# Norm and head projection of a dense attention joined in one block, chunk by chunk

## The chip, the cores and the metric

One core of one Trainium2 chip. The metric is the device time of one execution in microseconds (us). Engines: PE is TensorE, PEld its weight loads, DVE is VectorE, ACT is ScalarE, POOL is GpSimd, SP is SyncE, which here only issues DMAs.

## What is computed

Two transformer layers on x of 2 x 1024 tokens by 128 channels. In each, a condition vector gives shift, scale and gate for two parts, and each part adds its gated result to x. The first part of a layer is a dense attention of 16 heads of 8 dimensions, and it begins with what matters here:

```python
h = _layernorm(x, axis=-1) * (1 + ca) + sa
# layer 0: rotary attention
qkv = (x @ w_qkv.T + b_qkv)          # x is h here
q = elu(q) + 1; k = elu(k) + 1       # then the rotary turn of the pairs
# layer 1: causal attention
q = embedded @ Wq.T + bq; k = embedded @ Wk.T + bk; v = embedded @ Wv.T + bv
v = jnp.where(jnp.isnan(v), 0.0, v)
```

After them follow a windowed attention with a feed-forward part (layer 0) and a mixture of experts (layer 1).

## The kernel before

x lies with channels on the 128 partitions and the 2048 tokens along them, in four chunks of 512. `build` (L2181) runs: `prologue`, then for the first dense attention `layer_norm` (call at L2214), `project_heads` (L2215) and `attention` (L2216), then the windowed layers, then `causal_block` (L1599) with the same three calls (L1604, L1607, L1608), then the experts. Each of these functions is one block: all engines meet at its end before any begins the next.

`layer_norm` (L213). Per chunk: an average over channels as a matmul with a matrix of 1/128 (L236, all four chunks first), centring on DVE (L290), square on ACT (L266), variance per token by four one-column matmuls (L244), root on ACT (L270), reciprocal on DVE (L294), the reciprocal spread over the partitions by four matmuls with the identity (L252), rescale on DVE (L298), shift on ACT (L274), which writes h. The root needs another function table of ACT than an exponential: such a change is an ACT_TABLE_LOAD record. A float32 matmul stands in the trace as two records, so "x2" at L425 is one matmul.

`project_heads` (L364). SP loads the weights and the bias and then the rows of ones (L343); ACT asks for the three rotary tables (L464). PE, ACT and DVE begin with a wait for the weights. Then steps s = 0 to 7, each one half (q or k) of a chunk; every engine has its own order, written out, and takes its instructions strictly in it. PE: `project(s)` (L425), `swap_pairs(s-2)` (L434), on even s `project_v` (L439), on odd s `turn_v` (L447). In the rotary case DVE drains a projection twice (L515, then L516: a pair of ramps), ACT takes the exponential (L469), POOL adds (L559), PE swaps pairs, DVE multiplies by cosine (L522) and sine (L527), POOL adds (L563). The result, val, is split in three bf16 parts: hi on ACT (L478), the rest on DVE (`less_hi`, L531), mid on ACT (L482), lo on POOL (L567), each some steps behind the projection. In the second attention ACT drains the projection (`biased`, L473) and there are no ramps; DVE cleans the values (L545 to L549). The values' bias (L486) and their tokens-first copy (L492) are ACT's in both. Projections use banks 0 and 1 of PSUM, swaps 2 and 3, values 4 and 5, turned values 6 and 7.

The parts reach the attention through DRAM: SP stores hi, mid, lo of the first batch's first group once four steps of each are done (L413, L351), waits for all to land (L415) and loads the first operands (L416, L360). The rest of the stores follow in the attention's block. The attention's first matmul (L716) waits for those operands.

`ChunkNorm` (L1611) is the same norm with one method per instruction and chunk, used so far by the experts only.

## Time and profile before

| | |
|---|---|
| median of 3 runs | 1840.9 us (1837.91 to 1841.72) |
| the profiled execution's own time | 1846.47 us |
| its span, first to last instruction | 1844.7 us |
| mean granted TensorE clock | 0.919 of the full one |
| first norm | 15.2 to 31.4 us |
| rotary projection block | 31.7 to 80.0 us |
| first matmul of the first dense attention | 84.14 us |
| second norm | 951.9 to 970.4 us |
| second projection block | 970.6 to 1007.8 us |
| first matmul of the second dense attention | 1012.25 us |

All times are microseconds from the span's start. The span leaves out what lies around the instructions, so it is compared with the time of its own execution and not with the median. The timeline merges neighbouring instructions of one line: its second number is then the length of the whole group, and in brackets stands how long the engine was idle before it and what ended that.

### The profile page before, as it was taken

The numbers are of one execution on the slowest core, as the hardware profiler recorded it, in microseconds if no ns is written. First come the engines' busy times: TensorE is split into PE (matmuls) and PEld (weight loads), VectorE is DVE, ScalarE is ACT, GpSimd is POOL, SyncE is SP. The second block draws the span as 40 slices with busy tenths as digits, with TensorE's granted clock in tenths as the row PEclk, the third lists the DMA queues.
The fourth block names the chain that finished last, engine by engine and source line by source line (L and its number), as shares of the span: only waits on it lengthen the run. The fifth ranks groups of instructions, "written<-read, shape, count | busy, mean of one in ns | idle before, by whom it ended". The sixth has DMA issues, their size and how long they took to land. (4 is left out here: it accounts for less than half of the span.)

```text
span 1844.7 us, 29294 instructions
## 1 busy us (share of the span) xinstructions
PE 1571.4 (85%) x11008; PEld 858.9 (47%) x11008; DVE 1393.5 (76%) x1954; ACT 1194.9 (65%) x2308; POOL 623.7 (34%) x492
## 2 busy tenths in 40 slices
PE   6489999997689876799783899999985799999998
PEld 4112222222357653566551233333323578888886
DVE  3799999992677446775443999999944489999996
ACT  2338888886377742777424377777772577777776
POOL 1840000000477522775003222222222255555555
PEclk8769999999799978999786699999996899999999
DMA  2140000000111100111001401111002021111111
GB/s 73 60 128 19 18 19 19 18 2 9 58 33 33 28 21 18 29 31 33 1 1 51 145 19 22 21 22 22 4 7 72 1 69 44 44 47 47 47 47 52
DMA packets 66620, 66.04 MB, mean 36 GB/s; under 512 B 38920, under 2 KB 42632, under 8 KB 65968
## 3 DMA queue, kind: packets, MB, share of 16 engines
q1 hardware_dynamic: 65840, 61.94, 12.3%
q8 instruction: 88, 1.44, 0.3%
q10 hardware_dynamic: 576, 2.16, 0.3%
q14 instruction: 52, 0.43, 0.1%
q0 software_dynamic: 64, 0.07, 0.0%
HBM read 40.85 MB, written 14.81 MB: 30 GB/s over the span
## 5 line engine op out<-in xcount | busy, mean ns | idle before, releaser
L817 ACT ACTIVATE att_probs<-psum 128x512 f32<-128x512 f32 x1024 | 535.2, 604 | 202.9 <-PE psum L745 202.3
L828 DVE TENSOR_REDUCE att_neg_max<-psum 128x1 f32<-128x1024 f32 x512 | 600.9, 1219 | 45.1 <-PE psum L716 39.3
L716 PE MATMUL psum<-att_k_op,att_q_op 48*128 48x512 bf16 x1024 | 351.0, 409 | 56.2 <-DMA att_k_op<-qk_parts 34.6
L745 PE MATMUL psum<-att_q_op,att_k_op 50*128 50x512 bf16 x1024 | 314.2, 388 | 19.4 <-ACT att_probs L817 19.4
L1916 ACT ACTIVATE moe_hidden<-psum,moe_b 128x512 f32<-128x512 f32 x256 | 167.4, 690 | 83.2 <-PE psum L76 83.0
L69 DVE TENSOR_TENSOR moe_hidden_low<-moe_hidden,moe_hidden_high 128x512 fp32r<-128x512 f32 x192 | 203.9, 1110 | 5.3 <-ACT moe_hidden_high L1922 5.2
L763 PE MATMUL psum<-att_probs,att_v 128*32 128x512 f32 (+2 forms) x1664 | 203.4, 558 | 2.9 <-ACT att_sums L809 2.8
L745 PEld LDWEIGHTS psum<-att_q_op,att_k_op 50*128 50x128 bf16 x1024 | 78.2, 94 | 250.9 <-ACT att_probs L817 187.6
L904 POOL TENSOR_TENSOR att_diag<-att_probs,att_triangle 128x512 f32<-128x512 f32 x64 | 82.0, 1281 | 272.5 <-PE psum L766 176.6
L716 PEld LDWEIGHTS psum<-att_k_op,att_q_op 48*128 48x128 bf16 x1024 | 72.5, 95 | 180.7 <-DVE att_neg_max L828 120.5
L1977 POOL TENSOR_TENSOR moe_hidden_low<-moe_hidden,moe_hidden_high 128x512 fp32r<-128x512 f32 x64 | 94.8, 1482 | 167.2 <-ACT moe_hidden_high L1922 167.2
L1433 POOL TENSOR_TENSOR wl_qk<-wl_qk,wl_part 128x512 f32<-128x512 f32 x64 | 81.5, 1276 | 88.4 <-DVE wl_part L1367 88.4
L1972 POOL TENSOR_TENSOR moe_cur<-moe_cur,moe_term 128x512 f32<-128x512 f32 x64 | 105.8, 1653 | 13.9 <-DVE moe_term L2052 13.6
L74 PE MATMUL psum<-moe_hidden_high,moe_w_high 128*128 128x512 f32 x256 | 103.4, 404 | 5.9 <-DVE moe_hidden_low L69 5.9
L1922 ACT ACTIVATE moe_hidden_high<-moe_hidden 128x512 fp32r<-128x512 f32 x192 | 106.6, 625 | 0.0
L74 PE MATMUL psum<-moe_cur_high,moe_w_high 128*128 128x512 f32 x256 | 101.6, 397 | 0.0
L76 PE MATMUL psum<-moe_hidden_high,moe_w_low 128*128 128x512 f32 x256 | 100.9, 394 | 0.0
L75 PE MATMUL psum<-moe_hidden_low,moe_w_high 128*128 128x512 f32 x256 | 100.7, 393 | 0.0
L1384 DVE TENSOR_REDUCE wl_mx<-psum 128x4 f32<-128x512 f32 x64 | 44.1, 689 | 73.9 <-PE psum L1185 73.9
L76 PE MATMUL psum<-moe_cur_high,moe_w_low 128*128 128x512 f32 x256 | 99.9, 390 | 0.0
L75 PE MATMUL psum<-moe_cur_low,moe_w_high 128*128 128x512 f32 x256 | 99.7, 390 | 0.0
L893 POOL COPY att_v<-v_tok 128x256 f32<-128x256 f32 x16 | 6.4, 399 | 253.5 <-PE psum L763 253.4
(239 smaller groups left out, 2897.8 us busy)
## 6 DMA issues: line engine op xcount, KB each, us to landing
moe_spread_weights<-gate_rows SPq DMA_DIRECT2D x64, 256.0 KB, 3.2
wl_v_shift<-wl_v SPq DMA_DIRECT2D x62, 128.0 KB, 2.2
att_q_op<-qk_parts SPq DMA_DIRECT2D x32, 192.0 KB, 3.2
att_k_op<-qk_parts SPq DMA_DIRECT2D x32, 192.0 KB, 4.3
qk_parts<-att_hi SPq DMA_DIRECT2D x12, 256.0 KB
qk_parts<-att_hi SPq DMA_DIRECT2D x12, 192.0 KB
qk_parts<-att_mid SPq DMA_DIRECT2D x8, 256.0 KB
moe_w<-in_moe_w SPq DMA_DIRECT2D x2, 1024.0 KB, 8.5
```

Of the source, the lines that this page charges most:

```text
L69: return dve.tensor_tensor(dst, src, high.bitcast(F32), ALU.subtract)
L74: pe.matmul(out, w_high, x_high, start=start, stop=False)
L75: pe.matmul(out, w_high, x_low, start=False, stop=False)
L76: return pe.matmul(out, w_low, x_high, start=False, stop=stop)
L716: mm = pe.matmul(buf[:, half * CHUNK:(half + 1) * CHUNK], q_op[it % RING][at_rows(p, MAX_ROW), j, t * P:(t + 1) * P], k_op[it % RING][at_r ...
L745: pe.matmul(st_bank[e % 3], k_op[it % RING][at_rows(p, MAX_ROW + 2), j, t * P:(t + 1) * P], q_op[it % RING][at_rows(p, MAX_ROW + 2), j, ha ...
L763: last = pe.matmul(out[:, 0:full], stage_v[r][:, t, j, :], pr[:, 0:full], start=first_tile, stop=final and full == CHUNK, skip_group_check ...
L817: act.activation(probs[:, g % PB, h, :], st_bank[e % 3], ACT.Exp, scale=scale).then_inc(exp_done, 1)
L828: dve.tensor_reduce(neg[:, t, p, j:j + 1], ring[e % 2], AX.X, ALU.max, negate=True).then_inc(ring_free, 1)
L1916: act.activation(hidden[:, n % 2, f, :], k.psum[:, f, :], ACT.Gelu_apprx_tanh, bias=b1[:, e, f:f + 1]).then_inc(gelu_done, 1)
L1922: act.activation(hidden_high[:, n % 2, f, :], hidden[:, n % 2, f, :], ACT.Copy)\
L1972: pool.tensor_tensor(cur[:, at], cur[:, at], term[:, n % 2, :], ALU.add).then_inc(added, 1)
```

## The change

`project_heads` takes x and the scale and shift and calls a `ChunkNorm` itself; the calls of `layer_norm` ahead of both dense attentions go. So norm and projection are one block, twice. The weights, the rotary tables and the rows of ones are asked for at its head, beside the norm; the wait for the weights stands behind the norm's first pieces. Chunk 0 and most of chunk 1 are normed ahead of step 0; the rest of chunk 1 lies in steps 0 and 1, and chunks 2 and 3 lie between the steps up to 5. `project(s)` on even s waits for its chunk's shift. The norm takes banks 6 and 7, so the values go through bank 4 alone and the turned values through bank 5 alone. `ChunkNorm` moves up in the file as it is (its removed copy is cut below).

```diff
--- before.py
+++ after.py
@@ -315,6 +315,67 @@
                                              ALU.mult, ALU.add)
 
 
+class ChunkNorm:
+
+
+    def __init__(self, nc, k, tag, src, dst, room, banks, scale, shift):
+        self.k, self.src, self.dst, self.scale, self.shift = k, src, dst, scale, shift
+        self.d, self.sq, self.dev, self.inv = room
+        self.at = [slice(c * CHUNK, (c + 1) * CHUNK) for c in range(CHUNKS)]
+        self.tiles = [slice(4 * c, 4 * c + 4) for c in range(CHUNKS)]
+        self.bank = [k.psum[:, b, :] for b in banks]
+        (self.mean, self.centred, self.squared, self.var, self.rooted, self.inverse, self.spread, self.scaled,
+         self.shifted) = sems(nc, *(f"{tag}_{n}" for n in LN_SEMS))
+
+    def average(self, pe, c):
+        pe.matmul(self.bank[c], self.k.ones_mean[:, :], self.src[:, self.at[c]], start=True, stop=True)\
+          .then_inc(self.mean, 1)
+
+    def centre(self, dve, c):
+        dve.wait_ge(self.mean, c + 1)
+        dve.tensor_tensor(self.d[:, self.at[c]], self.src[:, self.at[c]], self.bank[c], ALU.subtract)\
+           .then_inc(self.centred, 1)
+
+    def square(self, act, c):
+        act.wait_ge(self.centred, c + 1)
+        act.activation(self.sq[:, self.at[c]], self.d[:, self.at[c]], ACT.Square).then_inc(self.squared, 1)
+
+    def variance(self, pe, c):
+        pe.wait_ge(self.squared, c + 1)
+        for t in range(4):
+            i = 4 * c + t
+            last = pe.matmul(self.bank[c][:, t:t + 1], self.sq[:, i * P:(i + 1) * P], self.k.ones_mean[:, 0:1],
+                             start=True, stop=True)
+        last.then_inc(self.var, 1)
+
+    def root(self, act, c):
+        act.wait_ge(self.var, c + 1)
+        act.activation(self.dev[:, self.tiles[c]], self.bank[c][:, 0:4], ACT.Sqrt, bias=self.k.eps[:, 0:1])\
+           .then_inc(self.rooted, 1)
+
+    def invert(self, dve, c):
+        dve.wait_ge(self.rooted, c + 1)
+        dve.reciprocal(self.inv[:, self.tiles[c]], self.dev[:, self.tiles[c]]).then_inc(self.inverse, 1)
+
+    def spread_inverse(self, pe, c):
+        pe.wait_ge(self.inverse, c + 1)
+        for t in range(4):
+            i = 4 * c + t
+            last = pe.matmul(self.bank[c][:, t * P:(t + 1) * P], self.inv[:, i:i + 1].broadcast_to([P, P]),
+                             self.k.ident[:, :], start=True, stop=True)
+        last.then_inc(self.spread, 1)
+
+    def rescale(self, dve, c):
+        dve.wait_ge(self.spread, c + 1)
+        dve.scalar_tensor_tensor(self.d[:, self.at[c]], self.d[:, self.at[c]], self.scale(c * CHUNK // SEQ),
+                                 self.bank[c], ALU.mult, ALU.mult).then_inc(self.scaled, 1)
+
+    def add_shift(self, act, c):
+        act.wait_ge(self.scaled, c + 1)
+        act.activation(self.dst[:, self.at[c]], self.d[:, self.at[c]], ACT.Identity,
+                       bias=self.shift(c * CHUNK // SEQ)).then_inc(self.shifted, 1)
+
+
 class OperandRing:
 
 
@@ -361,7 +422,7 @@
                              self.parts[which, b, g, p].rearrange("c d j t -> (c d) j t")).then_inc(self.loaded[r], 16)
 
 
-def project_heads(nc, k, tag, h, A, rotary, operands):
+def project_heads(nc, k, tag, x, h, scale, shift, A, rotary, operands):
 
 
 
@@ -380,6 +441,9 @@
 
         w = sb("w", [P, 3 * DIM])
         bias = sb("b", [P, 3])
+        norm = ChunkNorm(nc, k, f"{tag}_ln", x, h, (sb("centred_x", [P, TOK]), sb("square", [P, TOK]),
+                                                   sb("deviation", [P, TILES]), sb("inverse", [P, TILES])),
+                         [6, 7, 6, 7], scale, shift)
         val = sb("val", [P, NU, CHUNK])
         part = operands.part
         if rotary:
@@ -417,9 +481,9 @@
 
         @block.tensor
         def _(pe):
-            pe.wait_ge(w_in, 16 * len(loads))
-
             def project(s):
+                if s % 2 == 0:
+                    pe.wait_ge(norm.shifted, s // 2 + 1)
                 if s >= 2:
                     pe.wait_ge(drained if rotary else operand, s - 1)
                 pe.matmul(bank[s % 2], w[:, (s % 2) * DIM:(s % 2 + 1) * DIM], h[:, cols[s // 2]],
@@ -434,20 +498,26 @@
                 pe.matmul(bank[2 + s % 2], swap[:, :], val[:, s, :], start=True, stop=True).then_inc(swapped, 1)
 
             def project_v(c):
-                if c >= 2:
-                    pe.wait_ge(v_done, c - 1)
-                pe.matmul(bank[4 + c % 2], w[:, 2 * DIM:3 * DIM], h[:, cols[c]], start=True, stop=True)\
+                if c:
+                    pe.wait_ge(v_done, c)
+                pe.matmul(bank[4], w[:, 2 * DIM:3 * DIM], h[:, cols[c]], start=True, stop=True)\
                     .then_inc(v_ps, 1)
 
             def turn_v(c):
                 pe.wait_ge(v_done if rotary else v_clean, c + 1)
-                if c >= 2:
-                    pe.wait_ge(v_tok_done, c - 1)
+                if c:
+                    pe.wait_ge(v_tok_done, c)
                 for t in range(4):
-                    last = pe.transpose(bank[6 + c % 2][:, t * P:(t + 1) * P],
+                    last = pe.transpose(bank[5][:, t * P:(t + 1) * P],
                                         k.v_ch[:, c * CHUNK + t * P:c * CHUNK + (t + 1) * P], k.ident[:, :])
                 last.then_inc(v_turned, 1)
 
+            norm.average(pe, 0)
+            norm.average(pe, 1)
+            norm.variance(pe, 0)
+            norm.spread_inverse(pe, 0)
+            norm.variance(pe, 1)
+            pe.wait_ge(w_in, 16 * len(loads))
             for s in range(NU + 2):
                 if s < NU:
                     project(s)
@@ -457,12 +527,20 @@
                     project_v(s // 2)
                 if s % 2 == 1 and 3 <= s < NU + 2:
                     turn_v((s - 3) // 2)
+                if s == 0:
+                    norm.spread_inverse(pe, 1)
+                if s in (1, 3):
+                    c = (s + 3) // 2
+                    pe.wait_ge(norm.scaled, c - 1)
+                    norm.average(pe, c)
+                if s in (2, 4):
+                    norm.variance(pe, s // 2 + 1)
+                    norm.spread_inverse(pe, s // 2 + 1)
 
         @block.scalar
         def _(act):
             for dst, src in tables:
                 act.dma_start(dst, src).then_inc(tables_in, 16)
-            act.wait_ge(w_in, 16 * len(loads))
 
             def exp_low(s):
                 act.wait_ge(floored, s + 1)
@@ -483,16 +561,22 @@
 
             def v_bias(c):
                 act.wait_ge(v_ps, c + 1)
-                act.activation((k.v_ch if rotary else vraw)[:, cols[c]], bank[4 + c % 2], ACT.Identity,
+                act.activation((k.v_ch if rotary else vraw)[:, cols[c]], bank[4], ACT.Identity,
                                bias=bias[:, 2:3]).then_inc(v_done, 1)
 
             def v_tok(c):
                 act.wait_ge(v_turned, c + 1)
                 b, t0 = c // 2, c % 2 * 4
                 act.activation(k.v_tok[:, t0:t0 + 4, b * GROUPS:(b + 1) * GROUPS, :],
-                               bank[6 + c % 2].rearrange("p (t g c) -> p t g c", t=4, c=32), ACT.Copy)\
+                               bank[5].rearrange("p (t g c) -> p t g c", t=4, c=32), ACT.Copy)\
                    .then_inc(v_tok_done, 1)
 
+            norm.square(act, 0)
+            norm.root(act, 0)
+            norm.square(act, 1)
+            norm.root(act, 1)
+            norm.add_shift(act, 0)
+            act.wait_ge(w_in, 16 * len(loads))
             for s in range(NU + 4):
                 if s < NU:
                     (exp_low if rotary else biased)(s)
@@ -504,11 +588,15 @@
                     mid(s - 4)
                 if s % 2 == 1 and 3 <= s < NU + 2:
                     v_tok((s - 3) // 2)
+                if s in (1, 3, 5):
+                    norm.add_shift(act, (s + 1) // 2)
+                if s in (1, 3):
+                    norm.square(act, (s + 3) // 2)
+                if s in (2, 4):
+                    norm.root(act, s // 2 + 1)
 
         @block.vector
         def _(dve):
-            dve.wait_ge(w_in, 16 * len(loads))
-
             def ramps(s):
                 dve.wait_ge(projected, s + 1)
                 b = bias[:, s % 2:s % 2 + 1]
@@ -530,6 +618,12 @@
                 dve.wait_ge(hi_done, s + 1)
                 dve.tensor_tensor(val[:, s, :], val[:, s, :], of(part[0], s), ALU.subtract).then_inc(rest1, 1)
 
+            norm.centre(dve, 0)
+            norm.centre(dve, 1)
+            norm.invert(dve, 0)
+            norm.rescale(dve, 0)
+            norm.invert(dve, 1)
+            dve.wait_ge(w_in, 16 * len(loads))
             for s in range(NU + 4):
                 if rotary and s < NU:
                     ramps(s)
@@ -548,6 +642,14 @@
                     dve.wait_ge(sined, 2 * c + 2)
                     dve.copy_predicated(k.v_ch[:, cols[c]], same[:, cols[c]].bitcast(mybir.dt.uint32),
                                         vraw[:, cols[c]]).then_inc(v_clean, 1)
+                if s == 0:
+                    norm.rescale(dve, 1)
+                if s in (3, 5):
+                    norm.rescale(dve, (s + 1) // 2)
+                if s in (1, 3):
+                    norm.centre(dve, (s + 3) // 2)
+                if s in (2, 4):
+                    norm.invert(dve, s // 2 + 1)
 
         @block.gpsimd
         def _(pool):
@@ -1601,72 +1703,10 @@
         k.v_ch = a.enter_context(nc.sbuf_tensor("v_ch1", [P, TOK], F32))
         k.v_tok = a.enter_context(nc.sbuf_tensor("v_tok1", [P, SEQ_TILES, UNITS, 32], F32))
         k.att = a.enter_context(nc.sbuf_tensor("att1", [P, SEQ_TILES, UNITS, 32], F32))
-        layer_norm(nc, k, "ln2", k.x, h, part(1, 1), part(1, 0))
         with ExitStack() as ring:
             operands = OperandRing(nc, k, "att1", ring)
-            project_heads(nc, k, "plain", h, A, False, operands)
+            project_heads(nc, k, "plain", k.x, h, part(1, 1), part(1, 0), A, False, operands)
             attention(nc, k, "att1", 1.0 / float(np.sqrt(SEQ)), True, operands)
-
-
...
 def heads_and_experts(nc, k, A, part, h, store):
@@ -2211,8 +2251,7 @@
             with ExitStack() as ring:
                 operands = OperandRing(nc, k, "att0", ring)
                 with nc.sbuf_tensor("h0", [P, TOK], F32) as h:
-                    layer_norm(nc, k, "ln0", k.x, h, part(0, 1), part(0, 0))
-                    project_heads(nc, k, "rot", h, A, True, operands)
+                    project_heads(nc, k, "rot", k.x, h, part(0, 1), part(0, 0), A, True, operands)
                 attention(nc, k, "att0", 1.0 / float(np.sqrt(HEAD_DIM)), False, operands, lepe.convolve)
             residual_attention(nc, k, "res0", lepe)
         with scope(nc):
```

## Rows read from the trace of the kernel before

**Rows 1.** The page of the profile, part 1: busy time, share of the span, instructions.

```profile
PE 1571.4 (85%) x11008; PEld 858.9 (47%) x11008; DVE 1393.5 (76%) x1954; ACT 1194.9 (65%) x2308; POOL 623.7 (34%) x492
```

**Rows 2.** Timeline, first norm: start, us, engine, line, operation, idle before it.

```profile
18.02 0.63 ACT L266 ACTIVATE ln_square<-ln_centred_x 128x512 f32<-128x512 f32 x1 [13.33 <-DVE ln_centred_x L290]
...
20.07 1.28 ACT L270 ACT_TABLE_LOAD   x1
...
26.89 0.97 PEld L252 LDWEIGHTS psum<-ident,ln_inverse 128*128 128x128 f32 x8
...
28.09 0.75 DVE L298 SCALAR_TENSOR_TENSOR ln_centred_x<-ln_centred_x,mod,psum 128x512 f32<-128x512 f32 x1
```

**Rows 3.** Timeline, the rotary projection block, same columns.

```profile
31.69 0.33 SPq L410 DMA_DIRECT2D rot_w<-in_rot_w  x1
...
35.88 2.08 PE L425 MATMUL psum<-h,rot_w 128*128 128x512 f32 x2 [6.00 <-DMA rot_b<-in_rot_b]
...
38.07 0.75 DVE L515 TENSOR_SCALAR rot_tmp<-psum,rot_b 128x512 f32<-128x512 f32 x1 [7.40 <-PE psum L425]
...
40.15 0.75 DVE L515 TENSOR_SCALAR rot_tmp<-psum,rot_b 128x512 f32<-128x512 f32 x1 [0.67 <-PE psum L425]
...
57.32 1.13 PE L434 MATMUL psum<-rot_val,rot_swap 128*128 128x512 f32 x2 [1.47 <-POOL rot_val L559]
57.74 0.74 DVE L515 TENSOR_SCALAR rot_tmp<-psum,rot_b 128x512 f32<-128x512 f32 x1
...
62.21 0.74 DVE L515 TENSOR_SCALAR rot_tmp<-psum,rot_b 128x512 f32<-128x512 f32 x1
...
62.87 0.73 DVE L516 TENSOR_SCALAR rot_val<-psum,rot_b 128x512 f32<-128x512 f32 x1
...
66.25 2.07 PE L434 MATMUL psum<-rot_val,rot_swap 128*128 128x512 f32 x2 [3.16 <-POOL rot_val L559]
```

**Rows 4.** Windows: length, busy of PE PEld DVE ACT POOL, granted clock, DMA, GB/s.

```profile
50.00:66.00 16.00, 8.24 (x22) 3.10 (x22) 16.00 (x20) 8.01 (x14) 16.00 (x11) 0.89 0.04 12
```

**Rows 5.** Groups by line: first norm, then (from L522) the rotary block.

```profile
L298 DVE SCALAR_TENSOR_TENSOR ln_centred_x<-ln_centred_x,mod,psum 128x512 f32<-128x512 f32 x4 | 3.0, 738 | 1.1 <-PE psum L252 1.1
L274 ACT ACTIVATE h<-ln_centred_x,mod 128x512 f32<-128x512 f32 x4 | 2.9, 721 | 4.5 <-DVE ln_centred_x L298 4.5
...
L270 ACT ACTIVATE ln_deviation<-psum,eps 128x4 f32<-128x4 f32 x4 | 1.0, 249 | 0.0
L294 DVE RECIPROCAL ln_inverse<-ln_deviation 128x4 f32<-128x4 f32 x4 | 0.7, 178 | 5.5 <-ACT ln_deviation L270 5.5
...
L522 DVE TENSOR_TENSOR rot_tmp<-rot_val,rot_cos 128x512 f32<-128x512 f32 x8 | 11.0, 1369 | 0.6 <-POOL rot_val L559 0.6
...
L531 DVE TENSOR_TENSOR rot_val<-rot_val,att_hi 128x512 f32<-128x512 f32 x8 | 9.2, 1146 | 2.0 <-ACT att_hi L478 1.8
...
L482 ACT ACTIVATE att_mid<-rot_val 128x512 bf16<-128x512 f32 x8 | 5.0, 628 | 10.6 <-DVE rot_val L531 10.6
```

**Rows 6.** Timeline, norm and projection ahead of the second dense attention.

```profile
965.00 3.53 PEld L252 LDWEIGHTS psum<-ident,ln_inverse 128*128 128x128 f32 x16
...
967.17 0.75 DVE L298 SCALAR_TENSOR_TENSOR ln_centred_x<-ln_centred_x,mod,psum 128x512 f32<-128x512 f32 x1 [1.44 <-PE psum L252]
...
973.29 2.07 PE L425 MATMUL psum<-h,plain_w 128*128 128x512 f32 x2 [4.45 <-DMA plain_b<-in_plain_b]
...
975.46 0.69 ACT L473 ACTIVATE plain_val<-psum,plain_b 128x512 f32<-128x512 f32 x1 [5.09 <-PE psum L425]
...
987.76 0.66 ACT L478 ACTIVATE att_hi<-plain_val 128x512 bf16<-128x512 f32 x1
```

**Rows 7.** Timeline, the end of the rotary block: stores, last lo, operand load.

```profile
69.88 1.18 SPq L351 DMA_DIRECT2D qk_parts<-att_lo  x2
...
75.61 2.52 POOL L567 TENSOR_TENSOR att_lo<-rot_val,att_mid 128x512 bf16<-128x512 f32 x2
...
78.29 0.82 SPq L360 DMA_DIRECT2D att_q_op<-qk_parts  x2
```

48 lines of the change are left out of this document (removed).

## The prediction

> **What bounds the kernel now.** The page comes first: TensorE is busy 85% of the span [rows 1], but the change touches only two stretches of about 70 and 60 us, one ahead of each dense attention, and there no engine is busy throughout. So I read the timeline of those stretches, then the groups of instructions for durations, then the rows at the handover to the attention. The reader is to see three things. (1) The first norm is latency: small instructions of four engines in a chain [rows 2]. After it TensorE sits idle 6.00 us, and in the second dense stage 4.45 us, until the weights, asked for only at the head of the projection block, have landed [rows 3, 6]. (2) The rotary projection begins with steps of 2.1 to 4 us and ends with steps of 4.47 us (57.74 to 62.21), in which VectorE and GpSimd are both busy the whole time [rows 3, 4]. (3) The projection block ends with a transfer: the last stores are issued at 69.88, their landing is waited for until 78.29, and only then are the attention's operands asked for. GpSimd's last piece ends at 75.61 + 2.52 = 78.13, just before [rows 7]. So what counts is when the first batch's parts (steps 0 to 7) are ready for the stores; the later steps hide behind the landing.
>
> The profiled execution took 1846.47 us, 5.6 above the 1840.9 median; the sum is made in its microseconds and the difference put on the median. About 0.2% (3.7 us) is what a measurement of this kernel can tell from no change.
>
> **Heads: what is won.** Rotary. Average, centring and first square stay where they are: the square starts at 18.02 [rows 2]. The table load of the root, now behind the second square (20.07), moves behind the first: 18.7 to 20.0. Then root 0.25, reciprocal 0.18, spread to rescale 1.2 (26.89 to 28.09), variance of chunk 1 behind the spread 1.0, root(1) and shift(0) 0.25 + 0.72 [rows 2, 5]. So 20.0 + 0.25 + 0.2 = 20.45, spread issued until 21.5, variance until 22.5, root(1) until 22.8, shift(0) until 23.5. The weights, asked for at 15.2, need the 4.2 us that they need now (31.69 to 35.88 [rows 3]) and are there. Projection(0) at 23.5, and the first ramp 2.19 later (35.88 to 38.07 [rows 3]): 25.7, now 38.07, so 12.4 won. Bounds: all at half clock 11.5 (spread 2.17 instead of 1.2, 965.00 to 967.17 [rows 6]), all at full clock 13.5. Second stage, same chain from 951.9: the first biased drain falls between 961.9 and 964.5, now 975.46 [rows 6]; won 11.0 to 13.6, taken 12.2, the middle, since this stretch shows both clock levels. **Together 24.6.** Issuing weights and tables early costs nothing: SP, with its loads and the six rows of ones, is idle there, and ACT's three table issues, some 1.3 us by the 0.33 of the row at 31.69 and its like, end before its first square is due at 18.02; a copy late by x would only delay that square by x.
>
> **Inside the projection: what is paid.** Chunks 2 and 3 are now normed between the steps. Each engine takes its instructions in order, so the chain shift(c) -> projection is closed at every chunk, while now all of h lies ready. I walk from ramp to ramp, rotary (starts of a pair lie 0.66 apart, 62.21 and 62.87 [rows 3]).
> Step 0: now 2.08 (38.07 to 40.15); spread(1) stands in TensorE's queue ahead of projection(1), 0.97 of issue [rows 2]: 3.05.
> Step 1: ramp 0.74, exponential 0.63, shift(1) 0.72, projection(2) 1.13 (57.32 [rows 3]), handovers: 3.45. Centring(2), 0.7 on VectorE, lies beside it.
> Step 2: swap and values behind projection(2), estimated 0.8 each from the 1.13 less its fill, then value bias 0.7, table load 1.28, root 0.25, reciprocal 0.18, spread 0.97, projection(3) 1.13, handovers 0.2: 6.3. VectorE waits, since projection(3) stands behind spread(2) and that behind the reciprocal.
> Step 3: ramps 1.3, cosine 1.0 (0.7 alone to 1.37 beside GpSimd [rows 5]), sine 0.65, rescale(2) 0.74, shift(2) 0.72, projection(4) 1.13: 5.5.
> Step 4: ramps 1.3, cosine 1.0, sine 0.6, less_hi(0) 1.05; then on ACT, ahead of root(3), mid(0) 0.63 and the table load 1.28; root, reciprocal, spread, projection(5) 0.25 + 0.18 + 0.97 + 1.13, handovers 0.2: 8.6.
> Step 5: to the end of less_hi(1) 3.95, mid(1) and value tokens 1.05, shift(3) 0.72, projection(6) 1.13, handovers 0.2: 7.1.
> Step 6 has no norm: 4.47 as now, or down to 2.9 as GpSimd has no backlog; taken 3.6.
> Sum 37.6; now 24.14 (38.07 to 62.21 [rows 3]): **13.5 paid**. To it comes the clock. In step 4 TensorE has nothing from variance(3) to spread(3), about 3.9 us, and after an idle 3.16 us the pair of matmuls at 66.25 took 2.07 where the one at 57.32 took 1.13 [rows 3]. I put spread(3) and projection(5) at half clock: 1.0 + 0.95 = **2.0**. Bounds 0, and 6 if every norm matmul and projection of steps 2 to 5 on the path falls so.
> Second stage (no exponentials: the root's table stays, no load is added), from one biased drain to the next, by the same kind of chain with ACT pieces at 0.5 to 0.6 when they stand behind one another. Step 0: values at half clock, spread and projection(1), 1.9 + 1.1 + 1.1 = 4.1. Step 1: drain, shift, projection, 0.7 + 0.7 + 1.1, and centring's handovers 0.5 = 3.0. Step 2: values, variance 0.8 + 0.7, root 0.25, reciprocal 0.18, spread, projection 0.97 + 1.13 = 4.0. Step 3: drain, hi, value tokens, shift on ACT 2.4, projection 1.13 = 3.55. Step 4: values 0.85, hi(1), mid(0), root(3) 1.4, reciprocal, spread, projection 2.28, the value drain and handovers 0.65 = 5.2. Step 5: drain, hi, mid, tokens, shift 2.85, projection 1.13 = 4.0. Then value bias and hi(3) 2.05, where the stores begin. Sum 25.9; now 975.46 to 987.76 + 0.66 = 12.96 [rows 6]: **12.9 paid**. Its idle gaps of TensorE stay near 1 to 2 us, so no clock term; bounds 0 and 4.
>
> Four more table loads (two before roots, two before exponentials) cost 1.28 each [rows 2]; the two before exponentials lie in ACT's wait for the next ramp and cost nothing, unless ACT is late there, then 1.28 each. Values in one bank cost nothing: bias(c-1) has drained the bank two steps before values(c); without that cover each would wait 0.7. The joined block saves one barrier, contained in the absolute times. After lo(3) the stores, landing and loads are the same, and GpSimd ends before SP can even ask for the operands [rows 7].
>
> A load took 1.28 us in the row (20.07), with the root 1.30 behind it, and the walk uses that. The Trainium skill's page ScalarE: Activation LUTs (What ACT_TABLE_LOAD costs, and Table sets) wants activations grouped by table set and budgets about 2.7 us for every switch, drain included. It speaks against this interleaving; by its figure the two loads on the path would cost 2.8 us more. The row shows half the figure, so the page's direction is kept, its size not.
>
> Sum: -24.6 + 13.5 + 2.0 + 12.9 = **+3.8 us**: 1844.7.
>
> **Rivals.**
> A, faster: the stalls thin out the work, so VectorE and GpSimd no longer slow each other. The cosine takes 1.37 in the mean and less_hi 1.15 [rows 5], and about 0.7 either would take alone; in steps 4 to 6 that gives back 3 x (0.7 + 0.45) = 3.5. With it, and no half clock, and nothing else: 3.8 - 3.5 - 2.0 = -1.7; with heads at full clock another 2.5 off: -4.2, 1836.7. For it: both engines are full in 50 to 66 [rows 4]. Against: ACT's and TensorE's chain, not VectorE, ends steps 2 to 5. Chance 0.14.
> B, slower by the clock: TensorE runs at half clock (1.2 GHz) through steps 2 to 5 of both stages, deciding wherever its gap reaches 3 us. Price 6 - 2 = 4 more in the first, 4 in the second: +11.8, 1852.7; one stage alone 1848.7. For it: the matmuls at 66.25 and the spread at 965.00 are at half clock [rows 3, 6]. Against: over 50 to 66, with TensorE busy 8.24 of 16 us, the granted clock is still 0.89 of the full one [rows 4]. The Trainium skill's page TensorE: Matmul & The Clock Gate (What's actually happening) has 1.2 GHz as the state to which an idle TensorE falls back; by that rule, the trace agrees (2.07 against 1.13). Chance 0.16.
> C, the change is hidden: the stores' landing (8.4 us) is set by the queue and not by their issue, or the shifts of steps cancel; within 0.2%. Chance 0.1.
> D, ACT is the late one: the loads before exponentials are not hidden, 2 x 1.28, and the two roots wait as long again: +3.8 + 2.6 to 5.1, 1847 to 1850. Chance 0.1.
>
> **How the numbers follow.** The forecast has 0.5, its own range is 0 to +7 us (1841 to 1848), cut by the 3.7 about in the middle: 0.27 within, 0.23 slower. B 0.16 and D 0.1 are slower, but a third of them, a small dose, ends within: 0.09. A is 0.14 faster, C 0.1 within. Sum: faster 0.14, within 0.46, slower 0.40. The range takes in the forecast, most of A and B with one stage, and the bounds of the heads (2.5) and the clock: 1837.5 to 1852.
>
> **What would show it.** Right: first ramp at about 25.7; ramps of steps 2, 3 and 5 apart by 6, 5.5 and 7 us; VectorE idle before them on TensorE; six table loads where now two are; the first operand load of the attention 3 us later in the first stage, under 1 later in the second. Wrong if step 4 takes under 6 us (A) or over 10 (B, D), if the first ramp is later than 28, or if the attention's first matmul moves otherwise than the eighth ramp.

## The result and the profile after

| | before | after |
|---|---|---|
| median of the runs | 1840.9 us (1837.91 to 1841.72) | 1850.21 us (1847.71 to 1855.74) |
| ratio, 95% interval | | 1.0059 (1.0039 to 1.0078) |
| the profiled execution's own time | 1846.47 us | 1847.71 us |
| its span | 1844.7 us | 1845.9 us |
| first matmul, first dense attention | 84.14 us | 89.65 us |
| second norm's first matmul to second attention's first | 60.34 us | 59.87 us |

The change makes the kernel slower, by 9.3 us on the medians and by 0.59% of 1841, 10.9 us, by the ratio. The forecast was 3.8 us slower, so its size was 5.5 us too small. The measured time lies in the stated range (1837.5 to 1852), and "slower" had 0.40 against 0.46 for "within 0.2%".

The two profiled executions differ by only 1.2 us. This pair understates the change: the one before is a long one of its kind and the one after the shortest of its five. So single spans are compared here only stretch by stretch, and totals by ratios.

The page of the kernel after, part 1, answers to [rows 1]; it tells as little as it did then.

```profile
PE 1578.2 (85%) x11008; PEld 861.1 (47%) x11008; DVE 1387.5 (75%) x1954; ACT 1200.8 (65%) x2312; POOL 622.3 (34%) x492
```

The timeline of the first stage after (start, us, engine, line, operation, idle before and what ended it) answers to [rows 2] and [rows 3]. L603 is the first ramp of a step, L489 the projection, L364 the spread, L353 the root.

```profile
23.53 2.04 PE L489 MATMUL psum<-h,rot_w 128*128 128x512 f32 x2 [1.05 <-ACT h L375]
...
25.69 0.75 DVE L603 TENSOR_SCALAR rot_tmp<-psum,rot_b 128x512 f32<-128x512 f32 x1 [2.70 <-PE psum L489]
...
30.16 0.75 DVE L603 TENSOR_SCALAR rot_tmp<-psum,rot_b 128x512 f32<-128x512 f32 x1 [0.39 <-PE psum L489]
...
49.31 1.28 ACT L353 ACT_TABLE_LOAD   x1
...
51.14 2.07 PE L364 MATMUL psum<-ident,rot_inverse 128*128 128x128 f32 x8 [3.73 <-DVE rot_inverse L358]
...
53.00 1.92 PE L489 MATMUL psum<-h,rot_w 128*128 128x512 f32 x2
...
54.96 0.75 DVE L603 TENSOR_SCALAR rot_tmp<-psum,rot_b 128x512 f32<-128x512 f32 x1 [3.87 <-PE psum L489]
...
60.45 2.08 PE L489 MATMUL psum<-h,rot_w 128*128 128x512 f32 x2 [3.28 <-ACT h L375]
...
66.17 0.74 DVE L603 TENSOR_SCALAR rot_tmp<-psum,rot_b 128x512 f32<-128x512 f32 x1
```

The reader is to see the first ramp at 25.69 (it was 38.07), and step 4, from 44.94 to 54.96: ACT's table load at 49.31, then spread and projection in a row at half clock (2.07 and 1.92 us; in step 2, at full clock, 1.16 and 1.02), with VectorE idle 3.87 us in front of the ramp. Between 25.7 and 66.2 VectorE waited 14.4 us for projections, 3.7 for roots and 1.9 for a spread.

The same timeline at the handover, SP's queue and the attention's first matmul, answers to [rows 7]:

```profile
66.08 3.67 SPq L412 DMA_DIRECT2D qk_parts<-att_hi  x6
...
71.41 2.40 SPq L412 DMA_DIRECT2D qk_parts<-att_mid  x4
...
73.85 1.18 SPq L412 DMA_DIRECT2D qk_parts<-att_lo  x2
...
83.76 0.82 SPq L421 DMA_DIRECT2D att_q_op<-qk_parts  x2
...
89.65 1.04 PE L818 MATMUL psum<-att_k_op,att_q_op 48*128 48x512 bf16 x4 [16.55 <-DMA att_k_op<-qk_parts]
```

and in a second profile of the kernel before (experiment e0):

```profile
60.76 3.67 SPq L351 DMA_DIRECT2D qk_parts<-att_hi  x6
...
70.03 1.18 SPq L351 DMA_DIRECT2D qk_parts<-att_lo  x2
...
78.43 0.82 SPq L360 DMA_DIRECT2D att_q_op<-qk_parts  x2
```

The eighth ramp came 3.96 us later (66.17 against 62.21), the lo stores 3.97 later (73.85 against 69.88), but the operand loads 5.47 later (83.76 against 78.29). That difference is explained below: what counts is the first hi store.

The second stage after, which answers to [rows 6]; it begins at 954.30, 2.39 us later than before:

```profile
959.46 1.16 PE L364 MATMUL psum<-ident,plain_inverse 128*128 128x128 f32 x8 [0.67 <-DVE plain_inverse L358]
...
964.61 0.69 ACT L551 ACTIVATE plain_val<-psum,plain_b 128x512 f32<-128x512 f32 x1 [2.29 <-PE psum L489]
...
990.84 3.66 SPq L412 DMA_DIRECT2D qk_parts<-att_hi  x6
...
1014.17 1.04 PE L818 MATMUL psum<-att_k_op,att_q_op 48*128 48x512 bf16 x4 [18.56 <-DMA att_k_op<-qk_parts]
```

The first biased drain comes 10.31 us after the norm's first matmul (before 23.55), the hi stores 36.54 after it (before 36.53) and the attention's first matmul 59.87 (before 60.34; e0 59.86). Here the head's win of 13.2 us is spent to the last tenth by the time of the first hi store.

### The profile page after: what moved, and what is told of

The parts are those of the page before. It is cut to its first block and busy times, and to the rows that moved or that the text cites. A ratio compares the mean times of both kernels' runs of the same rounds, so it can differ in the third digit from the quotient of the medians.

```text
span 1845.9 us, 29282 instructions
## 1 busy us (share of the span) xinstructions
PE 1578.2 (85%) x11008; PEld 861.1 (47%) x11008; DVE 1387.5 (75%) x1954; ACT 1200.8 (65%) x2312; POOL 622.3 (34%) x492
## 5 line engine op out<-in xcount | busy, mean ns | idle before, releaser
L847 PE MATMUL psum<-att_q_op,att_k_op 50*128 50x512 bf16 x1024 | 314.2, 387 | 19.5 <-ACT att_probs L919 19.5
L1535 POOL TENSOR_TENSOR wl_qk<-wl_qk,wl_part 128x512 f32<-128x512 f32 x64 | 81.6, 1277 | 88.6 <-DVE wl_part L1469 88.5
```

The costliest lines, as they stand in the source:

```text
L847: pe.matmul(st_bank[e % 3], k_op[it % RING][at_rows(p, MAX_ROW + 2), j, t * P:(t + 1) * P], q_op[it % RING][at_rows(p, MAX_ROW + 2), j, ha ...
```

## Experiments

Each kernel ran with the kernel of before on the same chip. Ratios are to that one, with 95% intervals; stretches come from the profile of the run named.

### e0 and e1: both kernels once more

No edit.

> The kernel of before once more, as one of the kernels under test. The medians moved by 9.3 us while the two profiled executions differ by 1.2 us in span. If the profiled execution of before (span 1844.7, 1846.5 us) was only a long one of its kind, a second profile has a span near 1839 (time near 1841), with the difference spread over stretches that the change does not touch. If profiling itself lengthens the execution by 5 us, it comes out near 1844.7 again while its timed runs stay near 1841. Ratio to before: 1.000 within 0.001.

> The changed kernel once more. The chain theory (steps closed by the norm's chain cost more than the heads save) expects the first attention's first matmul again 5 to 6 us later than before and the second attention's start relative to its norm 0.5 us earlier than before, so about +2 to +5 in all. A rival, that something outside the two joined stretches became slower (a later phase of the clock or of transfers in the windowed layers), expects these two stretches as just said, but the time 9 us above before, with the excess in the windowed layers, the attentions or the experts.

Before: 1842.4 us, ratio 1.0007 (0.9992 to 1.0022), span 1840.9. The first profile of before was indeed a long one: from the first matmul of its first attention (L716) to the first score matmul (L745) it took 31.0 us, this one 29.2, and the experts' part 448.3 against 446.4. After: 1852.2 us, ratio 1.0059 (1.0038 to 1.0080), span 1852.6: the same ratio twice, so the loss is firm, and larger than the +2 to +5 us expected here.

The first attention begins at 90.09 (e0: 84.09), 6.0 us later. The second stage took 63.22 us from its norm's first matmul to the attention's, 3.4 more than in e0 and 3.35 more than in the first profile of the changed kernel. Of these 3.35, 2.57 are there at the first hi store (39.11 us after the norm's first matmul, for 36.54), and they come with TensorE's clock in the head, as the timeline of e1 shows; the other 0.8 lies behind the stores.

```profile
962.40 2.08 PE L364 MATMUL psum<-ident,plain_inverse 128*128 128x128 f32 x8 [0.57 <-DVE plain_inverse L358]
...
969.18 0.69 ACT L551 ACTIVATE plain_val<-psum,plain_b 128x512 f32<-128x512 f32 x1 [2.29 <-PE psum L489]
```

The spread took 2.08 us where the profile above had 1.16; the variances before and after it took 1.80 and 1.71 for 1.06 and 0.96. The first biased drain came 12.69 us after the norm's first matmul instead of 10.31. What decides between the two levels was not found.

The rival of e1, that something outside the two stages became slower, is not borne out: from the first attention's first matmul to the second norm's it is 866.4 us here and 864.7 in the profile after, for 867.8 and 867.3 in the two of before.

### e2 and e3: one stage joined at a time

```diff
 # e2: causal_block
+        layer_norm(nc, k, "ln2", k.x, h, part(1, 1), part(1, 0))
...
-            project_heads(nc, k, "plain", k.x, h, part(1, 1), part(1, 0), A, False, operands)
+            project_heads_apart(nc, k, "plain", h, A, False, operands)   # the old function
 # e3: build, the same for the rotary stage, and causal_block as changed
```

> Only the rotary stage is joined; the second dense attention has the separate norm and projection of before. Chain theory: the first stage carries the loss (+5.5 at its handover by the trace, of which the attention gives back about 2), the second nothing, so this is slower than before by 2 to 6 us and as slow as the full change within 1 us. Rival (the second stage or something behind it carries the rest): +2 to +3 here, and the other half with the second stage alone.

> Only the second dense stage is joined; the rotary one is as before. Chain theory: within 1 us of before (0.5 us faster by the trace: the steps have no table loads and no half clock). Rival: slower by 4 us or more, which would put the missing part of the 9 us here.

First only: 1850.0, ratio 1.0050 (1.0033 to 1.0067), +9.2 us; the first attention begins at 91.15. Second only: 1845.6, ratio 1.0019 (1.0005 to 1.0034), +3.5 us; the second stage took 62.67 us, again with the head at half clock (first drain after 12.70). The first stage carries most of the loss, more than the 2 to 6 us expected: its first attention begins 7.1 us later than in e0, where I had counted on 5.5, of which the attention was to give back 2. The second was expected within 1 us of before and is not free: up to the first hi store it loses nothing when its head runs at full clock and 2.6 us when not. Four of seven profiles with a joined second stage that is otherwise that of the change had the head at 12.7 (e1, e3, g2, g3), three at 10.3 (after, f4, and f2 at 10.20).

### f1: the norm ahead of the steps, in the joined block

```diff
-                         [6, 7, 6, 7], scale, shift)
+                         [4, 5, 6, 7], scale, shift)
 # tensor (scalar and vector likewise, in layer_norm's order)
-            norm.average(pe, 0)
-            norm.average(pe, 1)
-            norm.variance(pe, 0)
-            norm.spread_inverse(pe, 0)
-            norm.variance(pe, 1)
+            for c in range(CHUNKS):
+                norm.average(pe, c)
+            for c in range(CHUNKS + 1):
+                if c < CHUNKS:
+                    norm.variance(pe, c)
+                if c:
+                    norm.spread_inverse(pe, c - 1)
 # in the steps: no norm; project(2) also waits for the last rescale;
# values in banks 4 and 5, turned values in 6 and 7, as before
```

> The joined block with the weights asked for at its head, but all four chunks normed ahead of step 0 in the order of the old norm, and the values in two banks as before. Chain theory (the loss is what is interleaved, the gain is the weights' wait): projection(0) starts when TensorE has issued spread(3), about 30 us in the first stage against 35.9 before and some 17.5 us after the norm's start in the second against 21.4; the steps are as before. So 5 to 6 us won in the first stage, 4 in the second: 9 to 10 us faster than before, some 18 to 20 faster than the full change. Rival (the joined block itself, its early transfers or its memory layout is what costs): no faster than before.

1831.7, ratio 0.9945 (0.9928 to 0.9963): 10.1 us faster than before and about 21 faster than the full change. Timeline of its first stage:

```profile
29.80 1.91 PE L491 MATMUL psum<-h,rot_w 128*128 128x512 f32 x2
...
31.83 0.75 DVE L595 TENSOR_SCALAR rot_tmp<-psum,rot_b 128x512 f32<-128x512 f32 x1 [1.04 <-PE psum L491]
...
54.38 3.67 SPq L412 DMA_DIRECT2D qk_parts<-att_hi  x6
...
72.06 0.82 SPq L421 DMA_DIRECT2D att_q_op<-qk_parts  x2
...
77.80 1.04 PE L806 MATMUL psum<-att_k_op,att_q_op 48*128 48x512 bf16 x4 [14.85 <-DMA att_k_op<-qk_parts]
```

The projection starts at 29.8 (before 35.88) and the steps keep their old lengths (24.15 us to the eighth ramp; before 24.14). The second stage took 54.07 us. So joining the blocks and asking early is worth 12 us at the two handovers, and norming between the steps is what loses: this kernel differs from the changed one in that placement (and in the values' banks, which cost nothing, as shown below).

### f2: the spread behind the next projection

```diff
                 if s < NU:
                     project(s)
+                if s in (3, 5):
+                    norm.spread_inverse(pe, (s + 1) // 2)
...
                     norm.variance(pe, s // 2 + 1)
-                    norm.spread_inverse(pe, s // 2 + 1)
```

> The changed kernel with one thing moved: spread(2) and spread(3) stand in TensorE's queue behind projection(3) and projection(5) and not ahead of them. Chain theory: steps 2 and 4 of the rotary stage lose the spread and the projection from their path and last 4.1 and about 6 us where the change has 6.3 and 10.0, since only the reciprocal holds VectorE; 6 us won at the first stage's stores, and about 4 (steps 2 and 4, 2 each) in the second if ACT is not the next limit there; time 4 to 8 us below the full change. Rival (ACT's root with its table loads sets the steps anyway): under 2 us won.

1846.6, ratio 1.0020 (1.0010 to 1.0031): some 7 us below the full change's ratio. Steps 2 and 4 of the rotary stage lasted 4.11 and 6.06 us (expected 4.1 and about 6). The timeline shows the ramp right behind the reciprocal, and where part of it is given back:

```profile
39.59 0.18 DVE L358 RECIPROCAL rot_inverse<-rot_deviation 128x4 f32<-128x4 f32 x1 [1.40 <-ACT rot_deviation L353]
...
39.68 0.72 DVE L604 TENSOR_SCALAR rot_tmp<-psum,rot_b 128x512 f32<-128x512 f32 x1
...
57.87 1.26 PE L489 MATMUL psum<-h,rot_w 128*128 128x512 f32 x2 [2.35 <-ACT h L375]
...
59.17 0.75 DVE L604 TENSOR_SCALAR rot_tmp<-psum,rot_b 128x512 f32<-128x512 f32 x1 [2.45 <-PE psum L489]
```

Step 5 (51.25 to 59.17) lasts 7.9 us in place of 7.6 and ends on ACT's shift: the next projection still waits for chunk 3 of h. From the first to the eighth ramp it is 35.28 us for 40.48. In the second stage step 5 grows from 4.03 to 7.76 and eats the 4 us won in steps 2 and 4. TensorE's order costs about what I said; behind it stands the chain of the norm itself.

### f4: TensorE kept busy in step 4

```diff
                     norm.variance(pe, s // 2 + 1)
+                    if s == 4:
+                        for _ in range(4 if rotary else 0):
+                            pe.matmul(bank[6], k.ones_mean[:, :], x[:, cols[0]], start=True, stop=True)
                     norm.spread_inverse(pe, s // 2 + 1)
```

> The changed kernel with four matmuls of no use (their output is overwritten) on TensorE between variance(3) and spread(3) of the rotary stage, where it idles 3.7 us. If the half clock there costs what the forecast put on it, spread(3) and projection(5) take 1.2 and 1.1 instead of 2.1 and 2.0 and step 4 lasts 8.1 instead of 10.0, and projection(6) may follow at full clock, another 1.0: 2 to 3 us below the full change. If the useless matmuls delay what they stand ahead of, or the level falls regardless, 0 or slower by up to 1.

```profile
49.55 3.68 PE L540 MATMUL psum<-x_ch,ones_mean_sb 128*128 128x512 f32 x8
...
53.42 1.16 PE L364 MATMUL psum<-ident,rot_inverse 128*128 128x128 f32 x8 [0.19 <-DVE rot_inverse L358]
...
54.42 1.02 PE L489 MATMUL psum<-h,rot_w 128*128 128x512 f32 x2
...
55.48 0.75 DVE L606 TENSOR_SCALAR rot_tmp<-psum,rot_b 128x512 f32<-128x512 f32 x1 [2.11 <-PE psum L489]
```

With the four useless matmuls (L540), spread(3) took 1.16 and projection(5) 1.02, at full clock, and step 4 lasted 8.25 us in place of 10.02. So the half clock there costs 1.8 us; the forecast had 2.0. Step 5 stayed at 7.60. The first ramp of this run came at 28.04, and its step 2 lasted 7.05 us for 6.30, as in g2 (7.05), which has none of these matmuls: projection(3) took 1.77 there in both, for 1.02. The ratio, 1.0041 (1.0023 to 1.0059), is 3 us below the change's 1.0059, but the intervals overlap: shown is the step, not the total.

### f5: hi's stores later, in the kernel of before

```diff
-                sp.wait_ge(part_done, NU // BATCH)
+                sp.wait_ge(part_done, NU // BATCH + (1 if level == 0 else 0))
```

> The kernel of before, but in both stages the stores of hi wait for one more step (five instead of four); mid and lo as before. In the first stage of five profiles the operands were asked for 17.7 us after the first hi store in each, though the lo stores came 9.3 us after it in two of them and 7 to 8 in three. If the transfers' own length, counted from the first store, sets the landing, the hi stores, about 3.5 us later in the first stage and 2 in the second, move the first attention matmul by as much: 5 us slower in all. If the last store sets it, only what the queue pushes lo back counts, about 1 us in the first stage and 1 in the second: under 2 us slower.

```profile
64.76 3.67 SPq L351 DMA_DIRECT2D qk_parts<-att_hi  x6
...
70.92 2.15 SPq L351 DMA_DIRECT2D qk_parts<-att_lo  x2
...
82.44 0.82 SPq L360 DMA_DIRECT2D att_q_op<-qk_parts  x2
```

The first hi store came at 64.76, 4.0 later than in e0, and the loads at 82.44: 17.68 us after it, although the lo stores came only 0.9 later than in e0 (70.92 against 70.03). In the second stage the hi stores moved by 1.90 and the loads by 1.91. Ratio 1.0028 (1.0014 to 1.0042), 5.2 us, as expected if the landing is counted from the first store. The same 17.68 us (17.66 to 17.69) stands between first hi store and operand load in both stages of every profile of a kernel with these stores, while the lo stores stand 8.4 to 11.5 us ahead of the load. Divided by the 12 stores it is 1.47 us each, the start and the last landing counted in.

### g3: no table loads inside the steps

```diff
+class PlainRootNorm(ChunkNorm):
+    def root(self, act, c):
+        if c < 2:
+            return super().root(act, c)
+        act.wait_ge(self.var, c + 1)
+        act.activation(self.dev[:, self.tiles[c]], self.bank[c][:, 0:4], ACT.Identity, bias=self.k.eps[:, 0:1])\
+           .then_inc(self.rooted, 1)
```

> The changed kernel, but for chunks 2 and 3 of the rotary stage ACT leaves the square root out (it passes the variance through an Identity of the same size), so that no function table changes inside the steps: only the root of those chunks is not computed. A load is 1.28 us in each trace. If it is on the path once per chunk at that price, steps 2 and 4 of the rotary stage shorten by 1.3 each (6.3 to 5.0, 10.0 to 8.7), more in step 4 if TensorE's shorter pause keeps it at full clock: 2.5 to 4.5 us at the handover. By the 2.7 us a switch of the Trainium skill's page ScalarE: Activation LUTs (What ACT_TABLE_LOAD costs) the two steps would shorten by 2.7 each, 5.4 in all. If the loads are hidden, nothing changes.

The kernel leaves out the square root of chunks 2 and 3 in the rotary stage; the rest is as in the change.

```profile
49.74 0.25 ACT L384 ACTIVATE rot_deviation<-psum,eps 128x4 f32<-128x4 f32 x1
...
50.25 1.27 PE L364 MATMUL psum<-ident,rot_inverse 128*128 128x128 f32 x8 [2.30 <-DVE rot_inverse L358]
...
53.27 0.75 DVE L612 TENSOR_SCALAR rot_tmp<-psum,rot_b 128x512 f32<-128x512 f32 x1 [3.07 <-PE psum L498]
```

Step 2 lasted 5.08 us (change 6.30), so the load cost 1.22 there. Step 4 lasted 7.79 (10.02): 2.23 less, of which 1.28 is the load; TensorE's spread, 1.27 us for 2.07, was still at full clock after the shorter pause. The projection behind it was not (1.92). So one load is on the path per interleaved root, at 1.2 to 1.3 us. The Trainium skill's page ScalarE: Activation LUTs (What ACT_TABLE_LOAD costs) gives 1.28 us for the load and 1.38 for a drain with it, 2.66 for a switch. The trace agrees with the first figure; with the drain on the path too, step 2 would have shortened by 2.66, and it shortened by 1.22. The head of this run was 2.2 us later (first ramp 27.91), and its step 6 lasted 4.61 us for 3.61, which hides the gain in the total: ratio 1.0047 (1.0032 to 1.0063), not distinguishable from the change's.

### g4: the weights late again, norm ahead of the steps

```diff
 # sync, in f1
+            sp.wait_ge(norm.shifted, CHUNKS)
             for dst, src in loads:
                 sp.dma_start(dst, src).then_inc(w_in, 16)
 # scalar: the tables' issues moved behind the same wait
```

> The version with the norm ahead of the steps, but weights, bias and tables are asked for only once the last chunk is shifted, as before the change. If that version's gain (12 us at the two handovers) is the weights' wait and the overlap that it allows, this one is back at the kernel of before: within 1 us of it. If the joined block gives something by itself (no barrier, another order), 1 to 5 us of the gain stay.

```profile
31.41 0.33 SPq L475 DMA_DIRECT2D rot_w<-in_rot_w  x1
...
34.42 2.07 PE L492 MATMUL psum<-h,rot_w 128*128 128x512 f32 x2 [4.58 <-DMA rot_b<-in_rot_b]
```

1840.1, ratio 0.9998 (0.9981 to 1.0015). The first attention begins at 81.6, 3.8 us later than in f1, and the second stage takes 58.19 for 54.07, 4.1 more. So about 8 of f1's 12 us at the handovers are the weights asked for early (here TensorE again sits 4.58 us for a transfer of 3.0), with the overlap of projection(0) and the last shifts. Against e0 the two handovers together still look 4 us better; the ratio's interval reaches from -3.5 to +2.8 us, so whether the joined block by itself gives anything stays open.

### g1 and g2: the first portion's stores cut in two

```diff
+                if portion == 0:
+                    for p in range(2):
+                        rows = slice(p * 2 * HEAD_DIM, (p + 1) * 2 * HEAD_DIM)
+                        sp.dma_start(self.parts[which, b, 0, p, c].rearrange("d j t -> (d j) t"),
+                                     self.part[level][rows, which, b * SEQ:(b + 1) * SEQ])\
+                          .then_inc(self.stored[portion], 16)
+                    continue
```

> The version with the norm ahead of the steps, and each store of the first portion cut into its two groups of 16 rows, so that the outermost dimension of the destination is 16 and not 2. In the traces so far these stores move at a steady 50 GB/s with a DMA share of 0.13, which is 2 of 16 engines, and the operands are asked for 17.68 us after the first of them in every profile. The Trainium skill's page DMA: Bandwidth & Descriptors (Why a DMA increments its semaphore by 16) says that a transfer is spread over the largest number of engines up to 16 that divides the slowest dimensions, 2 here. If that is the cause, the 24 shorter stores are bound by their issue: at 0.45 to 0.6 us each 11 to 14.4 us, and 2 to land, so 13 to 16.4 instead of 17.7: 1.3 to 4.5 us won in each of two stages, 3 to 9 in all against the version without. Rival (the transfers are bound by something else, such as the writes to DRAM): the share stays at 0.13 and nothing is won, or the issues of 24 stores cost more than 17.7: slower.

> The changed kernel with the same cut of the first portion's stores. If hi's stores set the handover because two engines carry all of them, then with 16 engines the operand load waits for lo and its landing: the loads are asked for 13 to 16.4 us after the first hi store instead of 17.7, 3 to 9 us below the full change. Rival: no difference.

Timeline of g1, SP's queue and the attention's first matmul:

```profile
53.16 5.44 SPq L415 DMA_DIRECT2D qk_parts<-att_hi  x12
...
63.57 1.81 SPq L415 DMA_DIRECT2D qk_parts<-att_lo  x4
...
66.63 0.77 SPq L428 DMA_DIRECT2D att_q_op<-qk_parts  x2
...
72.36 1.04 PE L813 MATMUL psum<-att_k_op,att_q_op 48*128 48x512 bf16 x4 [10.63 <-DMA att_k_op<-qk_parts]
```

The windows from the first store to the landing (length, busy time of PE, PEld, DVE, ACT, POOL, granted clock, DMA share, GB/s) of the change and of g2:

```profile
66.10:83.70 17.60, 4.61 (x13) 1.74 (x11) 11.91 (x13) 7.60 (x13) 15.85 (x11) 0.72 0.12 45
```

```profile
69.00:81.00 12.00, 3.70 (x13) 1.46 (x11) 10.20 (x11) 6.03 (x11) 11.60 (x9) 0.72 0.28 66
```

g1: 1820.9, ratio 0.9900 (0.9882 to 0.9919), the fastest of all, 18 to 20 us below before. The loads are asked for 13.5 us after the first store in the first stage and 12.2 in the second, where it was 17.7. g2: 1842.3, ratio 1.0006 (0.9994 to 1.0019): the same cut is worth 9.8 us by the ratios (3 to 9 expected), as much as the change had lost. It does not make the change good: with these stores the norm ahead of the steps is still 19.5 us faster by the ratios (0.9900 against 1.0006), and the kernel of before with the cut stores was not run. The share of the DMA engines rose from 0.12 to 0.28 of 16 and the rate from 45 to 66 GB/s; 0.12 is two engines. The Trainium skill's page DMA: Bandwidth & Descriptors (Why a DMA increments its semaphore by 16 and not by 1) says that a transfer uses the largest number of engines up to 16 that divides the slowest dimensions, which was 2 for these stores and is 16 after the cut. The share of 0.12 agrees with 2; 0.28 shows more than two at work, but not how many. What bounds the stores now is mostly their issue: 24 at 0.45 us are 10.9 of the 12.2 us. And the end that counts has changed: in both stages of g1 and g2 the loads follow 3.06 or 3.07 us behind the first lo store (in g2's first stage 81.18 behind 78.11), wherever the first hi store lies. In g1's first stage the parts come late enough that the stores pause, so there it is 13.5 and not 12.2.

## Why the prediction was right, and where its size was off

The direction was forecast with 0.40, the range held, and the size was too small: +3.8 against +9.3 by medians. By its own steps, the first stage:

| | forecast | profile after |
|---|---|---|
| first ramp | 25.7 | 25.69 (28.0 in four of the seven profiles with the change's head) |
| steps 0 to 3 | 3.05, 3.45, 6.3, 5.5 | 4.47, 3.25, 6.30, 5.23 |
| step 4 with the clock term | 10.6 | 10.02 |
| steps 5, 6 | 7.1, 3.6 | 7.60, 3.61 |
| first to eighth ramp | 39.6 | 40.48 |
| second stage, steps 0 to 5 | 4.1, 3.0, 4.0, 3.55, 5.2, 4.0 | 4.35, 2.87, 3.87, 3.52, 5.06, 4.03 |

**Right.** The mechanism: heads win, every interleaved chunk closes the chain from shift to projection, and VectorE waits. f1 shows it from the other side and f2 piece by piece. The clock term (2.0; f4: 1.8), the table load at 1.28 on the path (g3: 1.22), six loads where there were two. Values in one bank cost nothing: in the rotary steps TensorE had no idle time before L503 but issue. The second stage: forecast +0.7 us, measured 0.0 at the first hi store with the head at full clock, 2.6 more without.

**Where luck helped.** The forecast's own part of the range ended at 1848; the measured 1850.2 lies in the part added for rival B, whose half clock came in other places than B had said. The first ramp at 25.69 agrees so closely only because this profile's head was at full clock.

**Its own signs.** Two of the signs that it had named for being wrong did show. Step 4 took 10.02 us, over the 10 it allowed, but its own sum had 10.6 there, so this sign contradicts the forecast rather than refuting it. The attention's first matmul moved by 5.51 us and the eighth ramp by 3.96; that is the first of the two terms below. A third was passed narrowly in f2 and f4: first ramp later than 28 (28.02 and 28.04).

**The first term mis-sized: the end point of the first stage.** The prediction wrote: "So what counts is when the first batch's parts (steps 0 to 7) are ready for the stores", and took the eighth ramp and lo(3) for it. The runs show that the first store decides, 17.68 us ahead of the loads (f5), since its queue never runs dry. That store waits for hi(3), which is taken in step 6, 2.88 us behind that step's ramp where it was 2.21, because ACT is late there; and since it lies in step 6, that this step became shorter (3.61 us for 4.47) brings it nothing. So the first hi store came 5.47 us later (66.08 against 60.61), not 3.96. In the second stage I had rightly measured to hi(3), for want of ramps. This is 1.5 us.

**The second: the clock in the heads and in the early steps.** Step 0 was priced at full clock, "spread(1) stands in TensorE's queue ahead of projection(1), 0.97 of issue"; it took 1.91 at half clock, and the step 4.47 for 3.05. The half clock of the heads stood in the bounds only (11.5 and 11.0 us won); it is the more frequent case, and the first ramp is then 2.2 us later, the first biased drain of the second stage 2.4. A later head is followed by a somewhat shorter step 0 (3.65 to 4.31 us in four profiles, 4.02 to 4.54 in the other three), so the two do not simply add. In the old order TensorE's four averages stand in a row ahead of the first spread, which was at full clock in every profile of that order (1.14 us); with two averages and then one-column matmuls it was so in three of seven. That the row of four is the reason is my reading; no run tests it alone.

**Sum.** The stages end at the first hi store, so they are compared there, by the means of the profiles whose code up to that point is the change's or that of before. First stage: 67.1 (after, e1, e2, g2) against 60.8 us (before, e0, e3), +6.3, forecast +3.1. Second, from the norm's first matmul: 38.3 (after, e1, e3, f4, g2, g3) against 36.6 (before, e0, e2), +1.7, forecast +0.7. The 3.2 missing in the first stage are 1.5 for the end point, 0.9 for the walk from ramp to ramp (step 0 1.4 and step 5 0.5 too low, the others together 1.0 too high), and the rest what half clock in heads and steps cost in some of these profiles. Together the stages lost 8.0 us where 3.8 was forecast. The total does not close as well: from the first attention's first matmul to the second norm's it is 861.8 to 866.6 us in the seven profiles with the norm among the rotary steps and 866.5 to 867.8 in four without (before, e0, e3, f5), 2.3 us less by the means, and why is not known. So the profiles make it about 6 us in all, and the timed runs 9.3 by medians and 10.9 (7.2 to 14.4) by the ratio. The losses of the stages are shown; the rest of the total stays open.

Of the rivals, B had the right kind and other places: the half clock is in the heads, in step 0 and at times in projection(3). Nor was it a matter of gaps of 3 us alone: TensorE's gap ahead of spread(2) was 1.78 us in the profile after and in f4 and g2 alike, the spread took 1.16 in all three, and projection(3) behind it took 1.02 in the first and 1.77 in the other two. A is refuted for steps 4 and 5: cosines there did fall to 0.68 us (less_hi stayed at 1.16), and it gave nothing, since ACT and TensorE end the steps; it holds for step 6 alone (3.61). C had the landing right, which is fixed by the queue, but counted from the first store, so it travels with that store and hides nothing. D is refuted: the two added loads ahead of exponentials ran at 37.40 and 50.89, over before the ramps at 39.71 and 54.96, and in steps 1 to 7 the exponential began at most 0.04 us behind its ramp's end. Only in step 0 a load stands between the two (1.38 us), and there it does in e0 too.

## What to carry to other kernels

Interleaving two chains on engines that run in order turns each handover between them into a wait on the path: before spreading a stage over the steps of the next, count the links from its first piece to the piece that the next step needs, and compare with the wait that one could remove alone by asking for the weights earlier. Find out which transfer ends a stage and what bounds its queue: where the transfers are slower than their issue and the queue never runs dry, the first one sets the time (here 17.68 us to the load), and where the issue bounds it or pauses, the last one does (3.07 us). And look at the DMA share beside the rate: 0.12 of 16 engines says that the shape of the transfer, not its bytes, is the limit; cutting it differently was worth 8 to 10 us, about as much as the best placement of the norm (f1, 10 us).

## What the runs showed that I had not expected

- 64 KB stores with an outermost dimension of 2 moved at 45 to 51 GB/s (1.47 us each, landing counted in), on 0.12 to 0.13 of the DMA engines. Cut to 16 rows each, twice as many stores landed 4 to 5 us sooner.
- The same head of a norm came at two speeds from one profile to the next, 25.7 or 28.0 us for the first ramp and 10.3 or 12.7 for the first drain of the second stage, with TensorE's level: one spread 1.16 or 2.08 us.
- In the first 25 us the granted clock of the windows doesn't fit the durations (1.00 over 18.5 to 22.0 us of g3 and f2, beside a spread of 2.08 us), so there the level is read from the durations.
- Profiles of one kernel differ by 3.8 us in span (1840.9 and 1844.7 for the kernel before) and by 6.7 (1845.9 and 1852.6 for the changed one), as much as the forecast effect or more. One pair of profiles can't give the size of such a change.
